# Heads in two halves of TensorE's rows, experts with the tokens stationary, and a new order of steps in a decoder layer

## The reference, cut to what matters

```
y = ln(x)                                       # 1: attention by distance, one head
x = x + softmax(-gamma * |y_i - y_j|^2) @ y
y = ln(x)                                       # 2: cross attention to 154 context rows
q, k, v = y@Wq.T+bq, ctx@Wk.T+bk, ctx@Wv.T+bv   # 16 heads of 8 features
x = x + softmax(q.k/sqrt(8) + slope_h*(i-j)) @ v @ Wo.T + bo
y = ln(x)                                       # 3: 8 experts, the best 2 of each token
mask = one_hot(top2(y @ router.T + rb)).sum()   # 0 or 1 for each token and expert
x = x + sum_e mask[:, e] * (y @ W_e.T + b_e)
```

## Time and profile before

| | |
|---|---|
| median of three runs | 182.98 us (182.34 to 184.85) |
| profiled execution, first to last instruction | 182.3 us; no time of its own is given beside it |
| PE, DVE, ACT, POOL busy | 173.4, 150.5, 105.8, 60.7 us |
| largest groups of DVE | maxima 48.6 us in 88 instructions, masking 15.1 us in 24 |
| largest groups of PE | experts 32.5 us in 256 records, maxima 25.2 us in 170, scores 21.6 us in 96 |

### The profile page before, as it was taken

How to read it: one execution, slowest core, us unless ns; L and a number is a source line. 1 busy time by engine, 2 the same in 40 slices (tenths; PEclk the granted TensorE clock), 3 DMA queues, 4 the chain that set the end, 5 groups by cost and what they waited for, 6 DMA issues and landing times.

```text
span 182.3 us, 4382 instructions
## 1 busy us (share of the span) xinstructions
PE 173.4 (95%) x1514; PEld 123.6 (68%) x1514; DVE 150.5 (83%) x433; ACT 105.8 (58%) x219; POOL 60.7 (33%) x123
## 2 busy tenths in 40 slices
PE   6999999999899998999999999999997999999894
PEld 2355785477766685545465467775677969899893
DVE  7827879989999999998998998987299389699552
ACT  3036995979857396969789678979834040110100
POOL 4789733302363143855410002004397400010000
DMA  4930071636266554543742000001400010010002
GB/s 99 335 153 0 4 213 50 176 103 192 79 162 162 156 161 129 159 125 92 198 130 62 14 7 12 8 5 50 192 4 0 4 58 2 16 45 0 32 0 86
DMA packets 20003, 15.84 MB, mean 87 GB/s; under 512 B 1621, under 2 KB 18133, under 8 KB 19833
## 3 DMA queue, kind: packets, MB, share of 16 engines
q1 hardware_dynamic: 19982, 15.57, 29.1%
HBM read 9.19 MB, written 6.37 MB: 85 GB/s over the span
## 4 chain that ended last, share of the span: by engine, by line
PE 72%; DVE 19%; issue 3%; ACT 3%; POOL 1%; ACTq 0%; DVEq 0%
PE bank L1440 15%; DVE nm L1091 9%; PE bank L1371 8%; PE bank L1344 7%; PE bank L1316 6%; PE bank L1214 6%; PE bank L1263 6%; PE bank L1210 5%; PE bank L1279 4%; DVE y L989 3%; PE bank L1421 3%; PE bank L1340 2%; PE bank L1367 2%; ACT w L857 2%; PE bank L1390 2%
## 5 line engine op out<-in xcount | busy, mean ns | idle before, releaser
L1091 DVE TENSOR_REDUCE nm<-bank 128x3 f32<-128x462 f32 (+1 forms) x88 | 48.6, 614 | 0.8 <-PE bank L1316 0.6
L919 ACT ACTIVATE pt<-bank 128x512 f32<-128x512 f32 x80 | 43.3, 604 | 3.8 <-PE bank L1344 2.7
L1440 PE MATMUL bank<-ewT,ym 128*128 128x128 f32 x256 | 32.5, 277 | 0.0
L1440 PEld LDWEIGHTS bank<-ewT,ym 128*128 128x128 f32 x256 | 30.3, 192 | 0.2
L1316 PE MATMUL bank<-ks,qs 99*128 99x308 bf16 (+1 forms) x170 | 25.2, 262 | 0.0
L1344 PE MATMUL bank<-qs,ks 105*128 105x256 bf16 (+1 forms) x96 | 21.6, 309 | 0.0
L1316 PEld LDWEIGHTS bank<-ks,qs 99*128 99x128 bf16 x170 | 15.1, 98 | 8.3 <-DVE nm L1091 2.2
L1186 DVE TENSOR_TENSOR ym<-bank,y3T 128x512 f32<-128x512 f32 x24 | 15.1, 684 | 4.9 <-PE bank L1421 4.9
L798 POOL TENSOR_SCALAR ve<-mv 128x2 f32<-128x2 f32 (+1 forms) x6 | 1.3, 210 | 50.2 <-DVE mv L984 50.0
L1371 PE MATMUL bank<-pt,vm 128*32 128x256 f32 (+1 forms) x192 | 17.3, 456 | 0.0
L1263 PE MATMUL bank<-y1Tg,y1T 128*128 128x512 f32 x32 | 16.6, 601 | 0.3 <-ACT y1Tg L837 0.3
(11 more groups left out here) (143 smaller groups left out, 287.8 us busy)
## 6 DMA issues: line engine op xcount, KB each, us to landing
ks<-k_scratch SPq DMA_DIRECT2D x4, 480.0 KB, 4.5
q_scratch<-qpart SPq DMA_DIRECT2D x8, 192.0 KB, 2.1
qs<-q_scratch SPq DMA_DIRECT2D x8, 192.0 KB, 3.4
xs<-in_x_dram SPq DMA_DIRECT2D x4, 256.0 KB, 4.2
q_scratch<-qpart SPq DMA_DIRECT2D x8, 128.0 KB, 2.4
qs<-q_scratch SPq DMA_DIRECT2D x8, 128.0 KB, 3.1
mask_all<-e_scratch SPq DMA_DIRECT2D x1, 1024.0 KB, 4.5
k_scratch<-mask_all SPq DMA_DIRECT2D x4, 240.0 KB, 2.6
```

The costliest lines, as they stand in the source:

```text
L919: nc.scalar.activation(pt[:, n % RING, :], at("scores", b, i)[:, :], ACT.Exp).then_inc(exps, 1)
L1091: v.tensor_reduce(nm[b][:, n:n + heads], at("maxima", b, g)[:, 0:heads * J].rearrange("p (s j) -> p s j", s=heads), AX.X, ALU.max, negate= ...
L1440: last = mm(at("experts", b, p)[:, tile(t)], ym[:, e, tile(t)], ewT[:, e, :], start=False, stop=(e == E - 1), skip_group_check=True)
```

## The change

**Heads in halves of the rows.** A head now has its own 64 partitions (0 to 63 or 64 to 127) and no zero rows: 51 rows are multiplied in `maxima`, 54 in `scores`. Matmuls come in pairs, one for each half, each with its own bank. A `maxima` step is three such pairs (six heads) and DVE reduces both banks with one instruction of 924 columns: 46 instead of 88. Each DMA of queries and keys becomes two, one per half. The keys' scratch tiles are half as large.

**Experts.** A tile of `y3T` is stationary, the weights of four experts (512 columns) are moving: two matmuls for a tile, with no mask. ACT (four activations of 128 columns with a scale for each token, 23 half tiles) or DVE (one instruction of 512 columns, 9 half tiles) multiplies with the mask from PSUM into a ring of four tiles, `zs`. The eight experts are then added by three instructions of 512, 256 and 128 columns, on POOL for 14 tiles and on DVE for two, and DVE adds that sum to `xs`, tile by tile (16 `store` steps). The bias has its own matmul and addition (`bias`, `biased`). Gone are `spread`, `select`, `eout`, `ein`, the load of `sel`, and the way of the mask over DRAM.

**Order.** All lists and `TURNS` are new. A step of `maxima` holds two adjacent banks. `q_rows` (six small DMAs) is issued ahead of the first `x`. `WARM` is 17 ahead of `y1T:0.0` and nothing else.

```diff
-MASKS = "psss"
+MASKED = ("aaavaaav", "aaavaaav", "aaavaaav", "aaavavav")
+SUMS = ("pppp", "pppp", "pppp", "ppvv")
+SLOTS = 4
 ...
-        x:0.0 gamma:0.0 x:1.0 x:2.0 k_rows:0.0 cols:0.0 x:3.0 context:0.0 weights:0.0 experts:0.0 k_rows:1.0
+        cols:0.0 q_rows:0.0 x:0.0 x:1.0 gamma:0.0 x:2.0 x:3.0 experts:0.0 k_rows:0.0 k_rows:1.0 context:0.0
 ...
-    "y1T:0.0": 28, "sqT:0.0": 4, "probs:0.0": 2, "y1T:3.0": 3, "maxima:0.0": 2, "probs:3.0": 4,
-    "scores:0.0": 1,
+    "y1T:0.0": 17,
 ...
+                for i in range(min(GROUP, entries(b) - n)):
+                    a, t = (n + i) // n_t, n_t * p + (n + i) % n_t
+                    for s in range(2):
+                        rows = slice(HALF * s, HALF * s + MAXROW)
+                        last[s] = mm(at("maxima", b, g, s)[:, i * J:(i + 1) * J], qs[b][rows, a, tile(t)],
+                                     ks[b // 2][rows, a, b % 2, 0:J], start=True, stop=True)
 ...
+            def sum_(b, t):
+                n = T * b + t
+                z = zs[:, n % SLOTS, :, :]
+                for i in range(2):
+                    pool.wait_ge(*z_masked(2 * n + i))
+                done(g.tensor_tensor(z[:, 0:4, :], z[:, 0:4, :], z[:, 4:8, :], ALU.add))
+                settle()
+                done(g.tensor_tensor(z[:, 0:2, :], z[:, 0:2, :], z[:, 2:4, :], ALU.add))
+                settle()
+                g.tensor_tensor(z[:, 0, :], z[:, 0, :], z[:, 1, :], ALU.add).then_inc(pool_summed, 1)
 ...
+            def masked(b, k):                                   # ACT
+                n = 2 * T * b + k
+                t = k // 2
+                if n // 2 < SLOTS:
+                    act.wait_ge(k_ready, 2)
+                else:
+                    act.wait_ge(out_ready, n // 2 - SLOTS + 1)
 ...
+                for i in range(E // 2):
+                    e = k % 2 * (E // 2) + i
+                    last = nc.scalar.activation(zs[:, n // 2 % SLOTS, e, :], at("experts", b, k)[:, tile(i)], ACT.Copy,
+                                                scale=picked[b][:, t, e:e + 1])
+                last.then_inc(act_masked, 1)
 ...
+                v.tensor_tensor(xs[b][:, t, :], xs[b][:, t, :], zs[:, n % SLOTS, 0, :], ALU.add).then_inc(out_ready, 1)
 ...
+            def experts(b, t):
+                for i in range(2):
+                    turn("experts", b, 2 * t + i)
 ...
+                    mm(at("experts", b, 2 * t + i)[:, :], y3T[b][:, tile(t)],
+                       ewT[:, i * (E // 2):(i + 1) * (E // 2), :].rearrange("p e n -> p (e n)"), start=True,
+                       stop=True).then_inc(z_ps, 1)
```

More of the change, by code:

```diff
@@ L80 @@
[L80 to L89, removed]
@@ L95 @@
[L95 to L98, removed]
+        table:0.0 y1T:0.0 sqT:0.0 dist:0.0 dist:0.1 dist:0.2 keys:0.0 keys:0.1 soft:0.0 soft:0.1 soft:0.2 probs:0.0
+        probs:0.1 probs:0.2 dist:0.3 y1T:1.0 soft:0.3 sqT:1.0 probs:0.3 y2T:0.0 sqT:2.0 dist:1.0 dist:1.1 query:0.0
@@ L124 @@
+        masked:2.3 biased:2.0 biased:2.1 wo:3.1 route:3.0 y3:3.1 store:2.0 store:2.1 masked:2.7 biased:3.0 route:3.1
+        masked:3.3 store:2.2 store:2.3 masked:3.5 sum:3.2 masked:3.7 biased:3.1 sum:3.3 store:3.0 store:3.1 store:3.2
+        store:3.3
     """,
     "tensor": """
-        start:0.0 y1T:0.0 sqT:0.0 dist:0.0 dist:0.1 dist:0.2 dist:0.3 keys:0.0 keys:0.1 key_values:0.0
-        probs:0.0 probs:0.1 self:0.0 self:0.1 y1T:1.0 probs:0.2 probs:0.3 sqT:1.0 self:0.2 self:0.3 sqT:2.0
-        y2T:0.0 sqT:3.0 dist:1.0 query:0.0 dist:1.1 y1T:2.0 dist:1.2 y2T:0.1 dist:1.3 query:0.1 dist:2.0
@@ L169 @@
+        aoT:3.0 y3T:2.1 experts:1.3 wo:3.0 scores:3.5 scores:3.6 scores:3.7 scores:3.8 bias:1.0 values:3.5 route:2.0
+        scores:3.9 values:3.6 values:3.7 route:2.1 experts:2.0 values:3.8 values:3.9 divide:3.2 y3T:3.0 mask:2.0
+        mask:2.1 divide:3.3 experts:2.1 aoT:3.1 bias:2.0 bias:2.1 route:3.0 wo:3.1 experts:2.2 experts:2.3 mask:3.0
+        y3T:3.1 experts:3.0 bias:3.0 route:3.1 experts:3.1 experts:3.2 mask:3.1 experts:3.3 bias:3.1
     """,
@@ L221 @@
[L221 to L227 removed]
+        y1T:0.0 dist:0.0 kp:0.0 vtp:0.0 dist:1.2 dist:2.0 probs:2.1 y2T:1.0 query:1.1 dist:3.1 probs:2.3
@@ new lines @@
+    """,
+    """
+        probs:0.1 probs:0.3 sqT:2.0 query:0.0 y2T:0.1 probs:1.0 self:1.0 probs:2.0 maxima:0.1 maxima:0.3
+        maxima:0.6 maxima:0.8 maxima:1.0 maxima:1.3 scores:0.5 maxima:1.6 maxima:1.8 maxima:1.10 maxima:2.0
+        maxima:2.1 maxima:2.4 scores:1.5 scores:1.8 scores:1.12 mT:2.0 scores:1.14 scores:1.16 divide:1.0
+        scores:2.2 divide:1.1 maxima:3.2 maxima:3.4 scores:2.13 scores:2.17 maxima:3.7 pv:3.0 maxima:3.9
+        experts:1.1 divide:3.1 scores:3.10 bias:1.0 scores:3.18 experts:2.1 mask:2.0 route:3.0 experts:2.6
@@ L228 @@
+    """,
+    """
+        probs:1.2 maxima:0.0 probs:2.2 maxima:0.4 self:2.0 probs:3.2 query:2.0 self:3.1 maxima:1.5 maxima:1.7
+        maxima:1.9 scores:0.17 maxima:2.3 scores:1.3 pv:1.0 scores:1.15 scores:1.19 scores:2.1 pv:2.0
+        experts:0.2 experts:0.5 maxima:3.6 divide:2.1 aoT:2.0 wo:2.0 scores:3.7 experts:0.6 divide:3.0
+        experts:1.0 y3T:2.1 scores:3.12 route:2.0 experts:2.0 divide:3.3 bias:2.0 experts:2.4 mask:3.0
+        bias:3.0 experts:3.3 experts:3.6
     """,
```

618 lines of the change are left out of this document (285 added, 333 removed).

## The result

The changed kernel takes 198.13 us (median of 4, 197.37 to 198.53) against 183.03 (182.34 to 184.85) for the kernel before, timed beside it: ratio 1.080 [1.073, 1.086]. The forecast was 170, the range 160 to 186. Both the size and the sign are missed. The profiled execution took 197.37 us; its span is 195.6, at a mean granted clock of 0.924 (before: 1.00 in every stretch of the earlier trace rows). In some executions of a kernel the clock stands lower and the time is longer than in its others; medians and ranges hold them all, ratios leave them out unless said otherwise.

What follows compares the result with a forecast made beforehand. PE and DVE were both taken as near full, the tail as PE's. PE: 182.3 - 16.0 - 1.0 (idle matmuls) + 1.9 (end) + 2.5 (start) = 169.7; DVE: 144.8 + 25.2 = 170.0. Forecast 170 us, range 160 to 186.

Steps and rivals of the forecast that it cites:

- +17 to +34 us over the run: SP queue: extra issue time of the doubled 24 `qin` and 24 `qout`, at half of 0.70 us to all of it.
- I expect the first maxima up to 2 us later, zero to 5: Start of batch 0's maxima: the delay expected because all 16 keys' DMAs stand ahead of its query loads on SP.
- DVE's sum: DVE over the run: work changes of -5.7 to 144.8 us busy, plus 25.2 idle, giving 170.0.
- PE's sum: PE's matmul work: experts -1.2, `spread` -5.3, scores -7.0, maxima -8.6, last keys' scores -1.7, changes of kind +7.8, together -16.0 us.
- The term of 0 to +4 (taken 2): Start: if the clock falls while PE waits for `y`, the first four `dist` matmuls run at half speed.
- the rival at 198 us: Clock stays low from 12 us to near 46, doubling some 30 us of PE work; chance 0.12 (over 187).
- the full overlap of pairs: Paired matmuls on the two row halves run together, halving scores, maxima and last keys' scores: 17.3 us gone from PE.
- The experts' 1.2: Experts on PE: 32 matmuls of 512 columns at 0.86 (27.5 us) replace 128 at 0.224 (28.7 us).
- Changes of kind: PE: switching between kinds of matmul costs 0.12 us each; 65 more switches add 7.8 us, zero to 15.6.
- the rival of the lock: DVE and POOL's shared ports: POOL's sums hold DVE 9.1 us, late stores keep slots, 178 us; chance 0.13 (175 to 179).
- theory L: Set up for the experiments: the new lists leave too much work behind the last query rows, whatever SP does.
- S: Set up for the experiments: SP's issue time, doubled by the cut, starves `maxima`; about 0.64 us for each DMA.

Runs made afterwards that it cites:

- Kernel 4: The kernel before with each query write and load cut in two DMAs, 48 DMAs more and the same bytes: 206.78 us, ratio 1.131.
- 1: The changed kernel with one query load for each half and all its copies, 16 loads instead of 48: 192.25 us, ratio 1.051.
- 5: Kernel 3 with the query DMAs of batches 1 to 3 merged over both halves of the columns, 8 a batch: 186.06 us, ratio 1.017.
- kernel 9: Kernel 5 with 17 idle matmuls instead of 44: 190.36 us, ratio 1.038.
- kernel 2: The changed kernel with all 44 idle matmuls of the kernel before: 197.45 us, ratio 1.072.
- kernel 8: The kernel before with only 17 of its 44 idle matmuls: 181.81 us, ratio 0.995.
- Kernel 15: Kernel 5 (44 idle matmuls) with batch 0's query rows in 2 loads and the keys of batches 2 and 3 behind them: 185.34 us, ratio 1.011.
- kernel 7: Kernel 5 with both halves of every pair on rows 0 to 63, so pairs run one after another: 207.72 us (196.04 to 216.62).
- kernel 11: Kernel 9 with batch 0's query rows in 2 loads, later keys behind them, and ACT's mask in one 512-column instruction instead of four: 190.68 us, ratio 1.047.
- 3: The changed kernel with kernel 1's merged query loads, 44 idle matmuls, and x and gamma ahead of q_rows on SP: 188.52 us, ratio 1.030.
- Kernel 12: The kernel before with only the change's experts, 44 idle matmuls, and the lists behind batch 3's scores made anew: 194.51 us, ratio 1.060.
- 14: The change's heads in halves with the old experts, merged query DMAs, 44 idle matmuls, lists and banks made anew: 199.57 us, ratio 1.093.

## Why the prediction was wrong

**The step that failed: SP.** The text has "+17 to +34 us over the run" for the doubled DMAs, and "half of 0.70 and all of it". The size was right: by the rows, a write and a load cost 0.64 to 0.75 and 0.73 for each half; 24 of each more make 33 us, the upper end. What failed is the next step: "I expect the first maxima up to 2 us later, zero to 5" (they came 9.9 later), "4.6 in the middle I leave at 5" in DVE's sum (20.6), and no term for SP in PE's sum. I followed the queue to batch 0's first load and stopped. Followed on, 18.2 us of issue for a batch, nearly without a gap, set when each batch's query rows can arrive. Kernel 4 shows it on the old code (+24 us); kernels 1 and 5 take it out of the new (5.9 us in 1; 12 in 5, together with the start and the idle matmuls). SP has no share of the chain before; that says that it had slack, not how much. From 29.5 to 95.7 us its issues take 47 of 66 us before, so that 19 were free, and these were never set against the 33.

The Trainium skill (DMA: Bandwidth & Descriptors, Rules for kernel authors) tells authors not to split a transfer over two halves of the partitions, since the two run one after the other, and to use one of 128 partitions. It spoke against this change and I did not weigh it. The trace agrees in direction, with +24 us in kernel 4, but puts the cost elsewhere: 0.73 us of issue for each on SP, while the DMA share in the middle stayed at 0.36, under the 0.40 of the earlier trace rows.

**The clock.** The term of 0 to +4 (taken 2) and the rival at 198 us were both about the start. The dips came behind waits of PE, at three places, and made matmuls longer: PE is busy 165.0 us against 161.2 in kernel 9 (clock 0.957), which has the same work and the same 17 idle matmuls. The rival named the measured time by chance: its mechanism, a clock that never rises from 12 to 46 us, did not happen (0.89 over 30 to 120), and kernel 2 shows that its cure brings some 2 us by itself. In the main the clock is a consequence of the waits (4, 8); how many idle matmuls lie across them matters too (9).

**PE's sum of -16.0** was too large. Kernels 5 and 15, with the 44 idle matmuls of the kernel before, have 161.7 and 162.3 us busy at a clock of 0.98, 11.7 and 11.1 under its 173.4; a part of the rest is the clock. The total looks right all the same: with 17 idle matmuls (5.7 us in the kernel after, 12.4 in 41 records in 5) it would be 155.0 against the forecast's 156.4. That is luck. The forecast had counted 1.0 for the idle matmuls; in kernel 8 PE is busy 5.3 us less without 27 of them, while the time falls by 0.9. Within the sum, the full overlap of pairs is right (kernel 7). The experts' 1.2 is wrong by its size: 0.91 for 512 columns, not 0.86, brings nothing. Changes of kind, 7.8 of the sum, were not measured by themselves.

**The base.** The span is 1.8 us shorter than the time of the same execution (195.6 and 197.37), so the 182.3 belongs to one of about 184, and a sum made on it gives a span. As a time, the forecast should have read 171.5. Beside the miss this is small.

**DVE's sum.** 148.4 us busy against 144.8. Maxima 46.5 against 44.6, in 46 instructions of 1.044 (1.05 forecast). Masking 6.2 against 5.6. If the rest, 1.1, is POOL's, its effect is 5.7 of the 9.1, where I took 4.6. DVE's and POOL's timeline after, which answers to the earlier trace rows:
```profile
149.37 0.60 DVE L989 TENSOR_SCALAR y<-xs,mv,rs 128x128 f32<-128x128 f32 x2
...
177.78 2.13 DVE L989 TENSOR_SCALAR y<-xs,mv,rs 128x128 f32<-128x128 f32 x2 [0.33 <-POOL rs L793]
...
177.76 1.26 POOL L800 TENSOR_TENSOR zs<-zs 128x512 f32<-128x512 f32 x1
```
Two of `y` in 0.60, and in 2.13 beside POOL's sum. So the rival of the lock is right in kind and small; the 5.7 is an estimate from a rest, not a measurement.

**DVE's idle time** is the other side of SP: 25.2 us forecast (11.2, 5 and 9), 47.2 measured (11.4, 20.6, 15.1). The start was right to 0.3 and for a wrong reason: PE's wait for `y` was 4.5, not 2.6. The tail's 9 is off by 6, and 6 us more idle PE than before stay there in 5 and 15, as in the kernel after; relieving the queue did not move them.

**Held:** ACT's new work is 25.5 us (24 forecast), and hidden (kernel 11). POOL's sums take 35.2 (31). Behind the last `divide` 24.5 us pass, under the 25 that "would sink the forecast".

**Chances.** The rivals had one of each kind, but none in which SP decides; it should have had a chance of its own. The sum was to be had from the earlier trace rows and the diff: 24 DMAs at 0.70 are 16.8 us for a batch and 67 for four; begun near 35 us, they end behind 102 even with no wait between them, where the kernel before had issued its last at 95.7 with gaps.

**What stays open.** SP made the change slower; that it is level and not faster once SP is relieved has other causes. Kernel 15 stands 15 us over the 170, and there theory L is not refuted. Its span of 183.1 is 13.4 over the 169.7: 5.9 in PE's busy time, near the 5.7 that its 27 more idle matmuls would cost at 0.21, and 7.5 in idle time. How long the work behind SP's last query load takes:

| | before | 4 | after | 1 | 3 | 5 | 15 |
|---|---|---|---|---|---|---|---|
| last query load issued, us | 95.7 | 116.3 | 115.5 | 105.6 | 101.7 | 99.5 | 98.6 |
| from there to the end, us | 86.6 | 87.4 | 80.1 | 84.8 | 84.0 | 84.3 | 84.5 |

The end follows the load, which is S. But with the load back near its old place, the new lists still need 84 us behind it, hardly less than the old ones, though PE has 11 us less to do. By the table above it is idle time of PE in many places, the largest at the end, where the chain of norm, route, mask, experts, mask, sum and store has to be walked for each tile. Kernels 12 and 14 were to divide it between experts and heads, and do not: each needed lists of its own, and neither run can tell the part from its list. What the best order for this change would give isn't known.

## What to carry to other kernels

- Count the DMAs of a queue, not their bytes: cutting one in two doubled its issue time here. Then set the queue's issue time for a batch against the batch's own time, through to the last batch.
- Forecast an engine's idle time in a sum of its own, with the reason of each piece: DVE's work was right here within 3% and PE's only by two slips that cancel, and the idle time was off by 17 us on PE and 22 on DVE.
- A wait on PE can cost twice, once for itself and once for the slower matmuls around it. Idle matmuls paid for themselves across waits (4.3 us in 9 against 5) and cost time where there were none (0.9 us in 8).

## What the runs showed of the hardware

- An issue of a strided half-size load takes 0.73 us on SP, one whose rows are contiguous over both halves of the columns 0.39 (0.78 for two, kernel 5), though it moves more.
- Pairs of bfloat16 matmuls on rows 0 to 63 and 64 to 127, all 128 columns, into two banks, run at the same time: three pairs of 154 columns in 0.20 us, 0.40 when both are on rows 0 to 63 (kernels 5 and 7, clock 1.00).
- The clock can be at 0.54 in a window in which PE was busy 8.63 of 10 us (100 to 110, after), right behind a stretch with waits, and at 1.00 through a kernel with 17 idle matmuls in which PE is idle 11.7 us in all but never waits longer than 1.5 (kernel 8).
- A comparison of 128 columns on DVE took 1.36 us beside POOL's sum of 512 columns, and 0.29 elsewhere. Kernel 12:
```profile
153.15 1.26 POOL L790 TENSOR_TENSOR ym<-ym 128x512 f32<-128x512 f32 x1 [1.14 <-ACT ym L949]
...
153.20 1.36 DVE L1147 TENSOR_TENSOR cmp_eq<-lg 128x128 f32<-128x128 f32 x1
...
176.24 0.29 DVE L1147 TENSOR_TENSOR cmp_eq<-lg 128x128 f32<-128x128 f32 x1
```
